# Attention output stage: two weight matrices around a norm multiplied together ahead of time, row scales applied last, four tiles per step

## What is computed

```python
out = outs.transpose(1, 0, 3, 2, 4).reshape(Bb, Ll, dm)      # rows of 256
out = _ln(out, post_w, post_b, eps=1e-05)
return out @ wo                                              # 256 x 256
```

## Time and profile before

| | us |
|---|---|
| median of 3 runs | 530.22 (527.67 to 531.71) |
| the profiled execution | 530.48 |
| its span in the profile | 528.6 |
| TensorE busy in the span | 414.5 (78%) |
| DVE busy | 327.2 (62%) |
| ACT busy | 285.2 (54%) |
| GpSimd busy | 194.5 (37%) |
| output stage | 67.7 |

### The profile page before, as it was taken

The page is one execution under the profiler, slowest core; times in us unless marked ns, Lnnn a source line. Parts: engine busy times, 40 slices in busy tenths (PEclk is TensorE's granted clock), DMA queues, the critical chain, the costliest instruction groups (busy, mean ns, idle before and its releaser), DMA issues. The chain is left out here.

```text
span 528.6 us, 10304 instructions
## 1 busy us (share of the span) xinstructions
PE 414.5 (78%) x3168; PEld 274.9 (52%) x3168; DVE 327.2 (62%) x1082; ACT 285.2 (54%) x694; POOL 194.5 (37%) x274
## 2 busy tenths in 40 slices
PE   0899968786458999999999349998298853885991
PEld 0455533221136777777877226776254333564981
DVE  4642131548425888888888333777749998538086
ACT  1243224754605666666666234666358882398544
POOL 0000000549032888888888470000442682000003
PEclk9999997797857999999999755999689967898996
DMA  7224440000021222222221333000000000000002
GB/s 191 41 58 136 139 135 14 1 0 0 0 71 32 57 68 60 60 60 65 62 69 43 106 85 82 1 2 0 1 1 0 1 0 15 7 1 1 0 1 79
DMA packets 35163, 23.05 MB, mean 44 GB/s; under 512 B 10286, under 2 KB 34876, under 8 KB 35132
## 3 DMA queue, kind: packets, MB, share of 16 engines
q1 hardware_dynamic: 34716, 22.55, 15.9%
q10 hardware_dynamic: 416, 0.13, 0.2%
HBM read 13.20 MB, written 9.47 MB: 43 GB/s over the span
## 5 line engine op out<-in xcount | busy, mean ns | idle before, releaser
L844 ACT ACTIVATE w_sb<-bank 128x256 f32<-128x256 f32 (+1 forms) x128 | 44.5, 400 | 0.0
L323 PE MATMUL bank<-w,hT 128*128 128x385 f32 x128 | 43.1, 490 | 1.2 <-ACT stage L356 1.0
L778 PE MATMUL bank<-w_sb,kqt 128*32 128x128 f32 x1024 | 43.1, 283 | 0.0
L576 POOL TENSOR_TENSOR turn<-xnT,coup 128x512 f32<-128x512 f32 x4 | 6.9, 1721 | 98.0 <-ACT coup L506 98.0
L323 PEld LDWEIGHTS bank<-w,hT 128*128 128x128 f32 x128 | 23.6, 189 | 20.8 <-issue 6.2
L1107 ACT ACTIVATE std_<-mv_,cst 128x2 f32<-128x2 f32 (+1 forms) x46 | 13.5, 296 | 36.7 <-DVE mv_ L1087 19.8
L379 DVE COPY stage<-bank 128x384 f32<-128x384 f32 x16 | 8.9, 558 | 36.0 <-DMA rows_scratch<-stage 32.9
L1320 POOL TENSOR_TENSOR win<-win,lng 128x512 f32<-128x512 f32 x2 | 2.5, 1266 | 77.1 <-ACT win L1601 77.1
L778 PEld LDWEIGHTS bank<-w_sb,kqt 128*32 128x32 f32 x1024 | 25.5, 110 | 7.9 <-issue 0.5
L913 POOL TENSOR_SCALAR xh<-raw,bmv,brs 128x128 f32<-128x128 f32 x32 | 25.4, 794 | 3.1 <-DVE brs L965 3.1
L773 PE MATMUL bank<-w_sb,cst 128*128 128x128 f32 x128 | 25.6, 282 | 0.7 <-DVE grad L1012 0.7
(11 more groups left out here) (294 smaller groups left out, 1246.2 us busy)
## 6 DMA issues: line engine op xcount, KB each, us to landing
rows_scratch<-stage SPq DMA_DIRECT2D x32, 192.5 KB
rows<-rows_scratch SPq DMA_DIRECT2D x32, 192.5 KB, 2.4
attn_scratch<-ob SPq DMA_DIRECT2D x32, 64.0 KB, 1.6
att<-attn_scratch SPq DMA_DIRECT2D x32, 64.0 KB
xt<-in_L_attn_x SPq DMA_DIRECT2D x4, 256.0 KB, 6.0
out<-win SPq DMA_DIRECT2D x4, 256.0 KB, 2.4
cst<-in_constants SPq DMA_DIRECT2D x1, 535.5 KB, 4.8
w<-in_L_attn_wk SPq DMA_DIRECT2D x2, 128.0 KB, 4.8
```

Source lines behind the costliest of these rows:

```text
L323: mm = nc.tensor.matmul(bank[4 + 2 * h + i % 2][:, 0:RC], hT[:, k, i * P:(i + 1) * P], w4[:, k, h, :], start=(k == 0), stop=(k == 1))
L778: mm = nc.tensor.matmul(dst[32 * b:32 * b + 32, 0:F], v[:, at:at + 2 * K], w_sb[:, state, first_slot(b) + h, :], start=False, stop=(h == 1 ...
L844: nc.scalar.activation(w_sb[:, state, at:at + n, :], bank[b][:, 0:n * F].rearrange("f (h g) -> f h g", h=n), ACT.Copy).then_inc(w_done, 1)
```

## The change

With post_w applied to `wo` and ln_w to `up`, the normed rows' product with `wo` is linear in the rows, and the mean over columns that the second norm subtracts is linear as well. The new kernel subtracts each row's mean over the columns from the weights themselves, and multiplies `wo` and `up` together once: `fold` holds for each of the 256 inputs the 256 columns of centred `wo` and the 128 columns of (centred `wo`) x (centred `up`), 384 (`RF`) in all. The output stage then multiplies the raw, transposed attention rows with `fold`; the bias comes with a matmul over four rows (the transposed standard deviations of four tiles against `fold_bias`, which holds one tile's row each). The second norm's variance is that of the first 256 columns, with a correction (`floor`) for the first norm's scale, and both norms' row scales are one multiplication (`rs2`) at the end. The feed-forward rows are turned and added to `xt` in the setup block.

Where things moved: `fold` is formed inside the loop over tiles of the input stage; the output stage runs by quarters of four tiles. In the diff, cut to its core:

```diff
                     for i in range(NT):
+                        if i == 8:
+                            column_sums()
+                        if i == 11:
+                            turn_fold()
+                        if i == 14:
+                            fold_up()
...
+                    def column_sums():
+                        pe.wait_ge(late_in, loads[late_in])
+                        pe.wait_ge(hT_done, 8)
+                        pe.wait_ge(folded, 3)
+                        for k in range(2):
+                            nc.tensor.matmul(bank[0][:, 0:HD], con("ones"), wo[:, k, :], start=(k == 0), stop=(k == 1))
+                        for k in range(2):
+                            nc.tensor.matmul(bank[0][:, HD:RF], con("ones"), up[:, k, :], start=(k == 0), stop=(k == 1))
+                        for k in range(2):
+                            nc.tensor.matmul(bank[1][0:B, 0:HD], post_b4[:, k, :], wo_raw[:, k, :], start=(k == 0), stop=(k == 1))
+                        for m in range(2):
+                            for k in range(2):
+                                nc.tensor.matmul(bank[1][:, HD + B * m:HD + B * (m + 1)], wo_raw[:, k, m * P:(m + 1) * P],
+                                                 post_b4[:, k, :], start=(k == 0), stop=(k == 1))
+                        for k in range(2):
+                            mm = nc.tensor.matmul(bank[1][0:D, RF:RF + 1], up_raw[:, k, :], ln_b[:, k:k + 1],
+                                                  start=(k == 0), stop=(k == 1))
+                        mm.then_inc(bias_mm, 1)
...
+                    def fold_up():
+                        pe.wait_ge(folded, 5)
+                        for k in range(2):
+                            for m in range(2):
+                                nc.tensor.matmul(bank[3][:, k * D:(k + 1) * D], mid[:, m, k * P:(k + 1) * P], up_c[:, m, :],
+                                                 start=(m == 0), stop=(m == 1))
...
@@ DVE, in its own loop over the tiles
+                        if i == 6:
+                            scaled_weights()
+                        if i == 9:
+                            centred_weights()
+                        if i == 12:
+                            dve.wait_ge(bias_mm, 2)
+                            nc.vector.tensor_copy(mid[:], bank[2][:, :].rearrange("p (m f) -> p m f", m=2)).then_inc(folded, 1)
...
@@ setup block
+                for b in range(B):
+                    for n in range(TPB):
+                        i = b * TPB + n
+                        mm = nc.tensor.transpose(bank[b][:, n * P:(n + 1) * P], g["ffnT"][:, i * P:(i + 1) * P], con("ident"))
+                    mm.then_inc(head_mm, 1)
...
+                for b in range(B):
+                    dve.wait_ge(head_mm, b + 2)
+                    rows_of = g["xt"][:, b * TPB:(b + 1) * TPB, :]
+                    ch.mark(nc.vector.tensor_tensor(rows_of, rows_of, bank[b][:, :].rearrange("p (n d) -> p n d", n=TPB), ALU.add))
...
@@ output stage, DVE
+                def row_stats(q):
+                    dve.wait_ge(at_in[q], 16 * B * H)
...
+                    for j in range(B):
+                        ch.mark(nc.vector.bn_stats(st[:, j, :], at[:, tile(q, j), :]))
+                    dve.wait_ge(stats, ch.n)
+                    for j in range(B):
+                        ins = nc.vector.bn_aggr(mv1[:, q % 2, j, :], st[:, j, :])
+                    ins.then_inc(var_done, 1)
+
+                def product_stats(q):
...
+                    for j in range(B):
+                        dve.wait_ge(mm_done, B * q + j + 1)
+                        ch.mark(nc.vector.bn_stats(st[:, j, :], bank[2 + j][:, 0:HD]))
+                    dve.wait_ge(stats, ch.n)
+                    for j in range(B):
+                        ch.mark(nc.vector.bn_aggr(mv2[:, j, :], st[:, j, :]))
+                    dve.wait_ge(stats, ch.n)
+                    nc.vector.tensor_tensor(var2[:], mv2[:, :, 1], floor[:], ALU.add).then_inc(var_done, 1)
+
+                def residual(q):
+                    dve.wait_ge(std_done, second_var(q))
+                    ch.link(nc.vector.reciprocal(rs2[:], std2[:]))
+                    for j in range(B):
+                        i = tile(q, j)
+                        nc.vector.scalar_tensor_tensor(out=xt[:, i, :], in0=bank[2 + j][:, HD:RF], scalar=rs2[:, j:j + 1],
+                                                       in1=xt[:, i, :], op0=ALU.mult, op1=ALU.add).then_inc(u_done, 1)
...
+                row_stats(0)
+                for q in range(TPB):
+                    product_stats(q)
+                    if q:
+                        next_scale(q - 1)
+                    if q + 1 < TPB:
+                        row_stats(q + 1)
+                    residual(q)
+                next_scale(TPB - 1)
...
@@ output stage, TensorE
+                def turn_stds(q):
+                    pe.wait_ge(std_done, first_var(q))
...
+                    nc.tensor.transpose(bank[6][0:B, 0:P], std1[:], con("ident")).then_inc(tr_mm, 1)
...
+                def products(q):
+                    pe.wait_ge(cp_done, max(copies["rows", q], copies["std", q]))
+                    for j in range(B):
+                        if q:
+                            pe.wait_ge(u_done, B * (q - 1) + j + 1)
+                        dst = bank[2 + j][:, 0:RF]
                         for k in range(2):
+                            nc.tensor.matmul(dst, attT[:, q % 2, j, k * P:(k + 1) * P], fold[:, k, :], start=(k == 0), stop=False)
+                        nc.tensor.matmul(dst, stdT[:, q % 2, :], fold_bias[:, j, :], start=False, stop=True).then_inc(mm_done, 1)
+
+                turn_rows(0)
+                turn_stds(0)
+                turn_rows(1)
+                products(0)
+                for q in range(TPB):
+                    if q + 1 < TPB:
+                        turn_stds(q + 1)
+                    if q:
+                        turn_normed(q - 1)
+                    if q + 2 < TPB:
+                        turn_rows(q + 2)
+                    if q + 1 < TPB:
+                        products(q + 1)
+                turn_normed(TPB - 1)
```

279 lines of the change are left out of this document (149 added, 130 removed).

## The result

| | before | after |
|---|---|---|
| median | 530.97 us (527.67 to 535.88) | 538.99 us (538.37 to 545.41) |
| ratio of the times | | 1.0184, 95% interval 1.0142 to 1.0225 |
| the profiled execution | 530.48 | 538.37 |
| its span | 528.6 | 536.5 |
| mean granted clock in the span | 0.889 | 0.878 |

The kernel became slower: by 8.0 us by the medians of all executions, and by 1.8% in the ratio, which leaves out one slow execution of the kernel before (535.88 us). The forecast had been 538.0 with a range from 527 to 552. That its total came true does not say that its parts did. So the span is cut at the five places where every engine waits for the others.

The account below looks back on a forecast made before the run. It took TensorE to bound the output stage, a copy loop waiting on DMA the input stage, and DVE's chain the setup's end. 2.7 + 2.8 + 2.3 = +7.8 us on 530.5 gave 538, range 527 to 552.

Parts of the forecast that it names:

- Part 1, the input loop: Input loop: products of the weights inserted ahead of tile 8 delay its copy and all later ones; +2.7 us.
- The third rival: Input loop: the DMA loop catches up and hides the inserted products, part 1 is 0, time 535; chance 0.13.
- Part 2, the setup block: Setup before the recurrence: four additions appended to DVE's chain of small operations; +2.8 us, between +2.3 and +3.4.
- Part 3, the output stage: Output stage: gaps between batches and a falling clock eat the shorter products' gain; 70.05 against 67.7 us, +2.3 us.
- head: Output stage's start: cold transposes, copies, root and quarter 1's transposes before the first product; 5.65 us.
- four batches at 2.4 GHz: Output stage: four batches of 24 product instructions on TensorE at full clock, 7.75 us each.
- three gaps: Output stage, between batches: no products run while DVE's statistics, root and transposes follow; 5.6, 6.7 and 5.2 us, 17.5 together.
- clock, within batches: Output stage: the clock falls in the gaps and batches start slow; 1.8 us for each of four, 7.2 us.
- tail: Output stage's end, after the last product: statistics, scale, residual, root, normalisations, transposes and copy; 8.7 us.
- 6 instructions of 384 columns at 0.32 us, 1.93 us: Output stage: TensorE's products per tile, two of the six for the four-row bias product, take 1.93 us.
- The first (the clock stays up): Output stage: the clock stays at 2.4 GHz through the gaps, stage 61.5 us, total 530, not slower; chance 0.17.
- The second (whole batches at low clock): Output stage: a batch wholly at low clock takes 15.5 us; 544 for one, 550 two, 562 all; chance 0.20.

Follow-up runs that it names:

- Experiment 5: Changed kernel with the five DVE operations that scale the weights run one tile sooner in the input loop; 541.54 us.
- Experiment 11: Kernel before, with ten unread transposes behind the setup's one matmul, ahead of the recurrence; 530.25 us, ratio 1.0002.
- experiment 6: Changed kernel with the next rows' statistics ahead of the products' and the bias product over 128 rows; 517.69 us, ratio to the kernel before 0.972.
- experiment 1: Changed kernel with the next rows' statistics and the last batch's scale ahead of the products' statistics on DVE; 524.21 us, ratio to the kernel before 0.9869.
- experiment 4: Changed kernel with five unread products on TensorE in each gap between batches of the output stage; 531.58 us.
- experiment 12: Kernel before, with its one-row bias product made over 128 rows, 127 of them zeros; 524.43 us, ratio 0.9877.
- experiment 3: Changed kernel with the setup's transposes and four additions ahead of the wait for the loads; 550.36 us in one execution.
- experiment 10: Changed kernel with the setup's transposes and additions first, the same kernel run again and timed; 543.57 us, ratio to the kernel before 1.0243.
- experiment 2: Changed kernel with the four-row bias product made over 128 rows, 124 of them zeros; 531.06 us in one execution.

## Why the forecast was right, and where it was not

**Part 1, the input loop: right, and shown.** Forecast +2.7, measured +2.5, and the copy of tile 8 late by 2.8 us against 2.6. Experiment 5 moved the wait by one tile and got back 1.33 us. The third rival (the loop catches up) did not happen: each microsecond at tile 8 is a microsecond at the end.

**Part 2, the setup block: right in its term, +2.4 for +2.8.** The four additions took 2.47 us. What was missed is the effect on the next stage: the transposes bring TensorE working to the recurrence, and it took 2.3 us less. Experiment 11 shows that on the kernel before, in the profile.

**Part 3, the output stage: right in sign, and mis-sized in one term.** By the forecast's own terms, forecast and measured (the stage's 73.3 us above include another 0.5 behind the tail's last operation):

| term, us | forecast | measured |
|---|---|---|
| head | 5.65 | 5.2 |
| four batches at 2.4 GHz | 31.0 | 37.1 |
| three gaps | 17.5 | 15.6 |
| clock, within batches | 7.2 | 6.0 |
| tail | 8.7 | 8.9 |
| sum | 70.05 | 72.8 |

The term that failed is "6 instructions of 384 columns at 0.32 us, 1.93 us". It took the four-row product's two instructions for two like the others. A tile took 2.33 us, and four batches 6.1 us more: 5.2 of that is the fee (9.27 against 7.98 in experiment 6), 0.9 what a batch takes beyond its 24 steps of 0.32 us (7.98 against 7.75). The rows held a warning that the forecast did not use: products of one row stood among full ones in the kernel before, and its turns came to 3.1 to 3.3 us, where the columns of the turn's 17 instructions come to some 2.5. Gaps and clock were overestimated by 1.9 and 1.2 us, which covered half of it. In the gaps TensorE was idle for 3.4 to 3.5 us, not 4.1, and the last gap, 4.11 us, lay below the 5 to 7 that had been announced and just above the 4 that would have counted against the forecast. The clock's sum came out near, but not its parts: 1.8 us had been put on each batch, and it was 1.0, 1.7, 0 and 3.4, so that three batches were longer than the 8 to 10 us announced. That the gap is DVE's chain, that the clock falls in it and that the whole costs more than the products save were all right, and experiments 1 and 4 show each by taking it away: 10.3 and 7.0 us, which overlap, since with shorter gaps the clock held in them too.

**The total was luck.** It came within 1 us because the stage's missing 2.6 us met 2.3 us that the recurrence gained and that no part of the forecast contains.

**Not forecast.** The feed-forward branch (-0.6) and the second layer (+1.0) hold no work of the change that could explain them. Over the kernels of the table they take 61.7 to 63.3 and 152.6 to 155.0 us, also where their code is that of the kernel before (experiments 11 and 12: 153.9 and 155.0), so both differences fit the scatter between kernels.

**The rivals.** The first (the clock stays up) did not happen in the change, and experiment 4 comes nearest to what it would have given, 531.6, where the forecast had put 530; but its output stage took 66.3 us where this rival had 61.5, so that nearness, too, owes something to the recurrence. The second (whole batches at low clock) got 0.20 for the reason that short products among full ones had been slow to rise before. It happened in experiments 3 and 10, once in each: in two of the six profiles with the four-row product and in none of the five with the wide one. But those two are of one kernel, with the setup's additions first, and no kernel has that together with the wide product and the row statistics in their old place, so the four-row product is not separated from the place of the additions. Nor did it delay the clock's first return in the changed kernel: 316.7 with it and 316.5 without (experiment 2). The reason given was a good one for the kernel before, as experiment 12 shows; that it is the cause of the cold batches is not proved.

**What stays open.** How far the clock's falls depend on where exactly work lies. The same code of the output stage took 73.3, 76.9, 80.1 and 81.4 us in four profiles of three kernels (after, experiments 5, 10, 3), which differ only ahead of it, so a total of this change is good to a few microseconds and no better.

## What to carry to other kernels

When a pipeline over tiles is made into batches, write down for each engine what it does while the other works; if the answer is "waits", the order of the statistics can matter more than the products saved, and a reordering can be worth the whole change (here 73.3 to 63.0 us). Make short operands full with zeros where they stand among full ones on TensorE: it was worth 1.2% on the kernel before, and on the changed one with the statistics first another 6.5 us. A repair upstream that shortens one block can cost the clock in the next, so judge it by the whole time.

## What the runs showed that was not expected

- A float32 product with an operand of four rows or one among full ones costs about 0.2 us at each change: 2.33 us a tile with it, 1.93 without (experiment 2), and the same 0.39 a turn in the kernel before (experiment 12). At each change the next weight load starts with its matmul instead of one matmul ahead. The Trainium skill, TensorE: Matmul & The Clock Gate, section "Why this matters for your kernels", says that a single matmul with 32 rows takes the time of one with 128. No run here has one alone; among full ones the measurement differs, and decides.
- With a one-row product in each turn the clock came back at 329 after 16 us of unbroken work; with 128 rows at 314.0 (experiment 12).
- In experiment 1 the clock fell 0.8 us into the fourth batch, after an idle piece of TensorE of 1.42 us; in experiment 6 it held behind one of 1.51 us at the same place. The first has the four-row product, the second the wide one; each is one execution.
- Transposes alone, ten of them ahead of the recurrence, went with a clock that was up 10 us sooner (experiment 11). In the changed kernel it rose at 156.3, behind the setup's product and sixteen transposes and before the recurrence's first matmul at 156.94.
